# A Swin pair on one core: image loads and stores issued from ScalarE instead of SyncE

## The chip, the cores and the metric

One Trainium2 chip, one core. The metric is device time in microseconds (us) of the whole program, as the median of several runs; beside it stands one profiled execution, whose rows are quoted below.

## What is computed

Two Swin transformer blocks are applied to 32 images of 192 channels and 32 x 32 pixels, float32, given and returned as (image, channel, row, column). Cut to what matters:

```python
x = x.transpose(0, 2, 3, 1)
shortcut = x
xn = layernorm(x)                                # over the 192 channels
xs = roll(xn, (-4, -4))                          # windows of 8 x 8 pixels
qkv = windows(xs) @ qkv_w + qkv_b                # 12 heads of 16
attn = softmax(q * 16 ** -0.5 @ k + bias + mask)
x = shortcut + roll(merge(attn @ v) @ proj_w + proj_b, (4, 4))
x = x + gelu(layernorm(x) @ fc1_w + fc1_b) @ fc2_w + fc2_b
```

The first block has the relative bias and the shift mask; the second has neither and is otherwise the same, with its own weights.

## The kernel before, in words

An image is held in SBUF as `x_img`, 96 partitions x 2 x 1024 float32, 768 KB; the finished image is gathered in `y_img`, of the same shape. The 1024 pixels make 8 tiles of 128 tokens (two windows each). There are 2 blocks x 8 tiles x 32 images = 512 visits of a tile, in groups of four, and `group_order` interleaves them: (image, block 0, first half), (previous image, block 1, first half), (image, block 0, second half), (previous image, block 1, second half). Every 16 visits the pattern repeats, with the next image.

The program is a software pipeline written out by hand. `run` (L253) calls a function `slot(s)` on each engine for s from -4 to 524; in slot s an engine works on several visits at different stages: the scores of visit s, the transposes of probabilities of s - 1, the projection of s - 3, the norm of s + 3 or s - 3, and a quarter of the MLP of an older group of four (`mlp_phase`, L100). Engines are tied by semaphores alone (`when`, L230: wait until stage `name` has been done for visit n), so they drift against each other: ScalarE and PE can be in slot s + 1 while SyncE is in slot s.

Between the engines run four DMA transposes per visit, all issued by SyncE (SP), in this order in each slot (L372 to L379): `qk_turn(s + 1)` (L369, q and k for the scores, tile `qkt`), `norm1_turn(s + 3)` (L346, `xt`, input of the qkv product), `norm2_turn(s - 3)` (L354, `ht`, input of the MLP), `o_turn(s - 1)` (L361, `ot`, input of the projection). Behind them, in two slots out of 16, stand the transfers of whole images: a load of the next image into `x_img` (L328), once POOL has copied the last tile of the present image out of it (`x_ordered`), and a store of `y_img` (L331), once ScalarE has put the last tile into it (`y_ready`). Those two are also in SP's one DMA queue.

On PE the scores of visit n begin at L485 (block 0) or L494 (block 1) and wait for `qkt`; the qkv product's q and k part is L436 with 384 columns and waits for `xt`; the v part is L469 and stands right ahead of the scores.

On ScalarE (ACT), slot s holds in this order: two or more GELUs in some slots, `norm2_hi` (L644), the copy of a new tile (L639), `v_hi` (L660), `p_hi` (L671), `y_evac` (L700, block 1's results into `y_img`), `exp` (L665), `qk_hi(s + 2)` (L651, two activations), and in every fourth slot GELUs around these.

POOL's `order_next` (L1065) is the reader of `x_img`: it waits for the load of its image and, four tiles in one group and four in another, copies it into windows.

Of the kernel before, what the change touches and what calls it, by code (L numbers as in the profile page):

```python
# [44 lines left out]
IMAGES, C, SIDE = 32, 192, 32  # L45
# [5 lines left out]
TILES = SIDE * SIDE // TOK  # L51
# [30 lines left out]
def visit(n):  # L82

    image, layer, half = GROUPS[n // GROUP]
    return image, layer, half * GROUP + n % GROUP


def rank(n):

    image, _, t = visit(n)  # L90
    return image * TILES + t
# [39 lines left out]
def swin_program(nc, x, layers, rel_bias, ident_in, q_mask_in, k_mask_in, out):  # L131
    H2 = C // 2
    with ExitStack() as ctx:
# [41 lines left out]
        x_img = sb("x_img", [H2, 2, SIDE * SIDE], F32)  # L175
# [51 lines left out]
        x_loaded = sem("x_loaded")  # L227
# [22 lines left out]
        def live(n):  # L250
            return 0 <= n < TOTAL
# [18 lines left out]
        @block.sync  # L270
        def _(sp):
            span = 2 * WS - 1

            def column(v, a, n):
                return v[a:a + n].rearrange("(c a) -> c a", a=1)

            def norm_columns(l, i, v):

                for dst, src in ((cols[:, l, i, 0:1], column(v, 0, 128)), (cols[0:CB, l, i, 1:2], column(v, 128, CB)),
                                 (cols[CB:128, l, i, 1:2], column(v, 0, CB)), (cols[:, l, i, 2:3], column(v, CB, 128))):  # L280
                    sp.dma_start(dst, src).then_inc(norm_in[l], 16)

            def weight_rows(j, v, n):

                for dst, src in ((stage[:, j % 2, 0, 0:n], v[0:128, :]), (stage[0:CB, j % 2, 1, 0:n], v[128:C, :]),
                                 (stage[CB:128, j % 2, 1, 0:n], v[0:CB, :]), (stage[:, j % 2, 2, 0:n], v[CB:C, :])):
                    sp.dma_start(dst, src).then_inc(w_in[j], 16)

            for l, L in enumerate(layers):
                for i, name in enumerate(("g1", "b1", "g2", "b2")):  # L290
                    norm_columns(l, i, L[name])
                for k, (name, n) in enumerate((("wqkv", 3 * C), ("wproj", C), ("wfc1", HID), ("wfc2", 0))):
                    j = 4 * l + k
                    if j >= 2:
                        sp.wait_ge(made, j)
                    if n:
                        weight_rows(j, L[name], n)
                    else:
                        sp.dma_start(stage[:, j % 2].rearrange("p a n -> p (a n)")[:, 0:HC * C]
                                     .rearrange("p (m c) -> p m c", m=HC),  # L300
                                     L[name].rearrange("(m p) c -> p m c", p=128)).then_inc(w_in[j], 16)
                    if k == 0:
                        for i, (bias, m) in enumerate((("bqkv", 3 * C), ("bproj", C), ("bfc2", C))):
                            o = (0, 3 * C, 4 * C)[i]
                            sp.dma_start(row[:, o:o + m], L[bias].rearrange("(a c) -> a c", a=1)).then_inc(w_in[j], 16)
                        sp.dma_start(vcol[:, 0:1], column(L["bqkv"], 2 * C, 128)).then_inc(w_in[j], 16)
                        sp.dma_start(vcol[0:CB, 1:2], column(L["bqkv"], 2 * C + 128, CB)).then_inc(w_in[j], 16)
                    if k == 2:
                        sp.dma_start(b_fc1[l][:, :], L["bfc1"].rearrange("(m p) -> p m", p=128),
                                     allow_slow_non_contiguous=True).then_inc(w_in[j], 16)  # L310
                    if j == 0:
                        sp.dma_start(ident[:, :], ident_in).then_inc(const_in[0], 16)
                        sp.dma_start(x_img[:, :, :], x[0].rearrange("(k p) h w -> p k (h w)", k=2)).then_inc(x_loaded, 16)
                    if j == 1:

                        for w in range(2):
                            for qr in range(WS):
                                src = bass.AP(tensor=rel_bias.tensor, offset=rel_bias.offset + qr * span * HEADS,
                                              ap=[[HEADS, WS], [span * HEADS, WS], [1, WS * HEADS]])
                                p0 = w * WIN + qr * WS  # L320
                                sp.dma_start(rel[p0:p0 + WS, :, :].rearrange("p (a b) h -> p a (b h)", a=WS), src)\
                                    .then_inc(const_in[2], 16)
                        sp.dma_start(q_mask[:, :], q_mask_in).then_inc(const_in[1], 16)
                        sp.dma_start(k_mask[:, :, :], k_mask_in).then_inc(const_in[1], 16)

            def load(image):

                sp.dma_start(x_img[:, :, :], x[image].rearrange("(k p) h w -> p k (h w)", k=2)).then_inc(x_loaded, 16)  # L328

            def store(image):  # L330
                sp.dma_start(out[image].rearrange("(k p) h w -> p k (h w)", k=2), y_img[:, :, :])\  # L331
                    .then_inc(y_stored, 16)

            when(sp, "x_ordered", TILES - 1)
            load(1)

            def slot(s):
                def ge(name, n):
                    when(sp, name, n)
                    sp.nop(nofuse=True)  # L340

                def norm1_turn(n):

                    ge("lo1", n)
                    ge("v_mm", n - 4)
                    sp.dma_start_transpose(xt[:, n % 4], xs[:, 0, n % 2].rearrange("p a c -> p (a c)"))\  # L346
                        .then_inc(LANDED["xt_in"][n % 2], 16)

                def norm2_turn(n):

                    ge("lo2", n)
                    ge("fc1", (n // GROUP - 2) * HC + HC - 1)
                    tok = slice((n % GROUP) * TOK, (n % GROUP + 1) * TOK)
                    sp.dma_start_transpose(ht[:, n // GROUP % 2, :, tok], xs[:, 1, n % 2].rearrange("p a c -> p (a c)"))\  # L354
                        .then_inc(LANDED["ht_in"][n % 2], 16)

                def o_turn(n):

                    ge("o_lo", n)
                    ge("pr", n - 2)  # L360
                    sp.dma_start_transpose(ot[:, n % 2], os[:, n % 2].rearrange("p a c -> p (a c)"))\  # L361
                        .then_inc(LANDED["ot_in"][n % 2], 16)

                def qk_turn(n):

                    ge("qk_lo", n)
                    ge("mask_set", n)
                    ge("s_mm", n - 2)
                    sp.dma_start_transpose(qkt[:, n % 2], qk[:, n % 2].rearrange("p h s d -> p (h s d)"))\  # L369
                        .then_inc(LANDED["qkt_in"][n % 2], 16)  # L370

                if live(s + 1):  # L372
                    qk_turn(s + 1)
                if live(s + 3):
                    norm1_turn(s + 3)
                if live(s - 3):
                    norm2_turn(s - 3)
                if live(s - 1):
                    o_turn(s - 1)  # L379
                if live(s + 10) and visit(s + 10)[1:] == (0, TILES - 1) and rank(s + 10) + 1 < IMAGES * TILES and s + 10 >= TILES:  # L380
                    ge("x_ordered", rank(s + 10))
                    load(rank(s + 10) // TILES + 1)
                if live(s - 9) and visit(s - 9)[1:] == (1, TILES - 1):
                    ge("y_ready", rank(s - 9))
                    store(rank(s - 9) // TILES)

            run(slot)
            sp.wait_ge(y_stored, 16 * IMAGES)
            sp.wait_ge(x_loaded, 16 * IMAGES)
# [239 lines left out]
        def _(act):  # L629
            copy = nc.scalar.activation  # L630
            act.wait_ge(made, 1 + 4 * LAYERS)

            def slot(s):
                def ge(name, n):
                    when(act, name, n)
# [56 lines left out]
                def y_evac(n):  # L692

                    image, _, t = visit(n)
                    ge("otr", rank(n))
                    if t == 0 and image > 0:
                        act.wait_ge(y_stored, 16 * image)
                    tile = ps_tr[0:H2, 0:2 * TOK].rearrange("p (k t) -> p k t", k=2)
                    for win, img in box_pairs(t, tile, y_img[:, :, :]):
                        last = copy(img, win, ACT.Copy)  # L700
                    last.then_inc(S["y_ready"], 1)
# [34 lines left out]
                    gelu(1)  # L736
                if last_block and place == 2:
                    y_evac(p * GROUP + 1)

            run(slot)  # L740


# [426 lines left out]
```

## Time and profile before

| | us |
|---|---|
| median of 3 runs | 4975.95 |
| lowest, highest run | 4972.98, 4988.05 |
| the profiled execution's own time | 4969.82 |
| its span | 4967.9 |

| engine | busy, us | share of the span |
|---|---|---|
| PE, matmuls | 4324.0 | 87% |
| PEld, weight loads | 3040.0 | 61% |
| DVE (VectorE) | 3374.5 | 68% |
| POOL (GpSimd) | 3008.3 | 61% |
| ACT (ScalarE) | 2772.6 | 56% |

A matmul counts as busy while it is in the pipeline, and weight loads overlap matmuls. The share is a mean over the span. Register, branch, semaphore and DMA-issuing instructions do not count as busy; the time of a DMA issue on SP stands in its own rows. A "wait" row names the instruction that ended an idle stretch.

### The profile page before, as it was taken

How to read it: one execution, taken by the hardware profiler on the slowest of the kernel's cores; microseconds unless marked ns; L12 is line 12 of the kernel's file. 1: busy time of each engine (PE TensorE's matmuls, PEld its weight loads, DVE VectorE, ACT ScalarE, POOL GpSimd, SP SyncE). 2: the span in 40 equal slices, each digit the busy share in tenths (PEclk: the TensorE clock that was granted, in tenths of full speed). 3: DMA queues.
4: the chain of work that ended last, by engine and by line, in shares of the span. 5: the costliest groups of instructions: out<-in, count | busy, mean ns of one | idle time of the engine just before them, and what ended most of it. 6: DMA issues, size and time to landing. Idle time of an engine off the chain costs nothing.

```text
span 4967.9 us, 174574 instructions
## 1 busy us (share of the span) xinstructions
PE 4324.0 (87%) x66384; PEld 3040.0 (61%) x66384; DVE 3374.5 (68%) x9081; ACT 2772.6 (56%) x5921; POOL 3008.3 (61%) x6254
## 2 busy tenths in 40 slices
PE   4888888988888988888889888888888888898987
PEld 2566665666666666666666666666566666666665
DVE  5666666767666767666666666766676666676765
ACT  1555555655555555555556555555555565555554
POOL 4666655666666666666566666665665665666654
PEclk9999999999999999999999999999999999999999
DMA  4444454445454444454454454444444544544442
GB/s 94 83 83 85 83 87 83 81 87 93 78 88 91 81 86 84 87 84 81 87 93 76 87 89 83 87 82 88 85 83 87 91 78 86 91 81 87 85 82 59
DMA packets 1467388, 420.49 MB, mean 85 GB/s; under 512 B 1450295, under 2 KB 1452731, under 8 KB 1466557
## 3 DMA queue, kind: packets, MB, share of 16 engines
q1 hardware_dynamic: 1466556, 409.32, 45.8%
q8 instruction: 532, 8.72, 0.7%
q14 instruction: 300, 2.45, 0.2%
HBM read 31.56 MB, written 25.17 MB: 11 GB/s over the span
## 4 chain that ended last, share of the span: by engine, by line
PE 46%; DMA 15%; DVE 10%; POOL 10%; issue 8%; SPq 8%; ACT 2%; POOLq 0%; DVEq 0%; ACTq 0%
PE ps_s L557 12%; DMA qkt<-qk 10%; PE bank L569 8%; PE bank L436 7%; PE bank L531 4%; POOL hid L1083 4%; DVE smax L880 3%; PE ps_t L514 3%; DMA xt<-xs 3%; DVE hid L918 3%; SPq L346 3%; PE ps_s L503 2%; POOL xs L1076 2%; PE bank L469 2%; PE ps_s L494 2%
## 5 line engine op out<-in xcount | busy, mean ns | idle before, releaser
L1022 POOL TENSOR_TENSOR rstd<-vare,half 128x2 f32<-128x2 f32 x518 | 360.1, 695 | 1081.2 <-DVE vare L858 1081.2
L918 DVE TENSOR_TENSOR hid<-hid 128x512 f16<-128x512 f32 x768 | 600.8, 782 | 528.5 <-POOL hid L1083 507.4
L557 PE MATMUL ps_s<-ht,w_fc 128*128 128x512 f16 x3840 | 878.7, 381 | 17.3 <-DMA ht<-xs 7.3
L569 PE MATMUL bank<-w_fc,hid 128*128 128x192 f16 x9216 | 851.0, 247 | 7.8 <-DVE hid L918 5.6
L880 DVE TENSOR_REDUCE smax<-ps_s 128x12 bf16<-128x768 f32 x512 | 488.2, 954 | 512.6 <-PE ps_s L494 499.7
L569 PEld LDWEIGHTS bank<-w_fc,hid 128*128 128x128 f16 x9216 | 774.1, 98 | 82.6 <-issue 55.9
L671 ACT ACTIVATE pt<-ps_t 128x768 f16<-128x768 f32 x512 | 415.4, 811 | 677.6 <-PE ps_t L514 674.6
L1083 POOL TENSOR_SCALAR hid<-hid 128x512 f16<-128x512 f32 x768 | 564.0, 734 | 310.6 <-ACT hid L679 309.1
L679 ACT ACTIVATE hid<-ps_s,b_fc 128x512 f32<-128x512 f32 x768 | 530.2, 690 | 342.4 <-PE ps_s L557 167.4
L557 PEld LDWEIGHTS ps_s<-ht,w_fc 128*128 128x128 f16 x3840 | 361.7, 98 | 459.9 <-issue 63.6
L436 PE MATMUL bank<-w_qkv,xt 128*128 128x384 f16 x2560 | 544.3, 346 | 47.6 <-DMA xt<-xs 45.2
L660 ACT ACTIVATE v_blk<-bank 64x192 f16<-64x192 f32 x1024 | 334.8, 327 | 325.7 <-PE bank L469 318.9
L651 ACT ACTIVATE qk<-bank 128x384 f16<-128x384 f32 x1024 | 447.8, 494 | 96.3 <-PE bank L438 93.8
L885 DVE TENSOR_TENSOR pt<-ps_t,pt 128x768 f16<-128x768 f32 x512 | 489.6, 956 | 16.3 <-issue 1.1
L665 ACT ACTIVATE p_tok<-ps_s 128x768 f32<-128x768 f32 x512 | 417.0, 814 | 134.4 <-PE ps_s L503 134.4
L514 PE MATMUL ps_t<-ident,p_tok 128*128 128x128 f32 x3072 | 487.7, 299 | 0.2 <-issue 0.2
L864 DVE SCALAR_TENSOR_TENSOR qk<-bank,qk 128x192 f16<-128x192 f32 x1024 | 316.6, 351 | 216.6 <-ACT qk L651 216.6
L644 ACT ACTIVATE xs<-xn 128x192 f16<-128x192 f32 x512 | 184.9, 361 | 450.2 <-POOL xn L1028 449.2
L436 PEld LDWEIGHTS bank<-w_qkv,xt 128*128 128x128 f16 x2560 | 256.8, 103 | 270.2 <-issue 129.6
L531 PEld LDWEIGHTS bank<-v_blk,pt 128*64 128x64 f16 x18432 | 332.9, 112 | 118.9 <-issue 118.9
L485 PE MATMUL ps_s<-bias_tab,pair_ident 128*128 128x384 f16 x512 | 142.0, 363 | 296.1 <-DMA qkt<-qk 282.6
L503 PE MATMUL ps_s<-smax,neg_ident 128*128 128x384 bf16 x1024 | 277.4, 355 | 132.5 <-DVE smax L880 129.3
(113 smaller groups left out, 7717.5 us busy)
## 6 DMA issues: line engine op xcount, KB each, us to landing
x_img<-in_x_dram SPq DMA_DIRECT2D x32, 768.0 KB, 5.9
out_dram<-y_img SPq DMA_DIRECT2D x32, 768.0 KB, 5.7
xt<-xs SPq DMA_TRANSPOSE x512
qkt<-qk SPq DMA_TRANSPOSE x512, 3.8
ot<-os SPq DMA_TRANSPOSE x512, 2.4
ht<-xs SPq DMA_TRANSPOSE x512, 2.3
stage<-in_L_conv_fc_w_dram SPq DMA_DIRECT2D x2, 384.0 KB, 4.0
stage<-in_L_conv_w_fc_dram SPq DMA_DIRECT2D x2, 384.0 KB, 4.5
```

The costliest lines, as they stand in the source:

```text
L436: last = mm(dst, blocks[:, blk, :], w[:, part, n0:n1], start=(i == 0), stop=(i == 4 and bias is None))
L514: last = nc.tensor.transpose(ps_t[:, g // 3, (g % 3) * TOK:(g % 3 + 1) * TOK], p_tok[:, n % 2, g].rearrange("p a k -> p (a k)"), ident[:, :])
L531: last = mm(ps_o[rows, g * 2 * VW:(g + 1) * 2 * VW].rearrange("p (a d) -> p a d", a=2), pt[:, n % 2, ps, g, rows], v_blk[:, n % 2, vs, :, ...
L557: last = mm(ps_s[:, u % 2, :], w_fc1[layer][:, part, m * 128:(m + 1) * 128], ht[:, p % 2, blk, :], start=(i == 0), stop=(i == 4))
L569: mm(bank[:, 0:C], hid16[:, hs, m, tok], w_fc2[layer][:, ws, m, :], start=(m == 0 and i == 0), stop=False)
L651: last = copy(qk[:, n % 2, i * HEADS:(i + 1) * HEADS, places, :], src.broadcast_to([128, HEADS, 2, HD]), ACT.Copy, scale=UNSCALE)
L665: nc.scalar.activation(p_tok[:, n % 2].rearrange("p g a k -> p a g k"), ps_s[:, :, 0:PAIRS * WIN].rearrange("p a (g k) -> p a g k", g=PAIR ...
L679: nc.scalar.activation(hid[:, u % 2, :], ps_s[:, u % 2, :], ACT.Gelu, bias=b_fc1[layer][:, m:m + 1], scale=UNSCALE).then_inc(S["gelu"], 1)
L880: v.tensor_reduce(smax[:, n % 2], ps_s[:, :, 0:PAIRS * WIN].rearrange("p a (g k) -> p a g k", g=PAIRS), AX.X, ALU.max).then_inc(S["max_don ...
L885: v.tensor_tensor(pt[:, n % 2, 1].rearrange("p (b g) t -> p b (g t)", b=2), ps_t[:, :, 0:3 * TOK], pt[:, n % 2, 0].rearrange("p (b g) t -> ...
L918: v.tensor_tensor(hid16[:, 1, m, :], hid[:, u % 2, :], hid16[:, 0, m, :], ALU.subtract)\
L1083: g_.tensor_scalar(hid16[:, 0, m, :], hid[:, u % 2, :], 1.0, 0.0, ALU.mult, ALU.add)\
```

## The change

`load` and `store` move from SP's program into ACT's, with the same transfers and the same semaphores. In ACT's slot they stand at the very end. A load is issued in the slot after the one that held it on SP (s + 9 in place of s + 10); a store in the slot of the same number. The first load inside the program, that of image 1 ahead of the loop, and that of image 0 stay on SP. SP still waits for all loads and stores at the end.

```diff
@@ SP @@
-            def store(image):
-                sp.dma_start(out[image].rearrange("(k p) h w -> p k (h w)", k=2), y_img[:, :, :])\
-                    .then_inc(y_stored, 16)
-
...
-                if live(s + 10) and visit(s + 10)[1:] == (0, TILES - 1) and rank(s + 10) + 1 < IMAGES * TILES and s + 10 >= TILES:
-                    ge("x_ordered", rank(s + 10))
-                    load(rank(s + 10) // TILES + 1)
-                if live(s - 9) and visit(s - 9)[1:] == (1, TILES - 1):
-                    ge("y_ready", rank(s - 9))
-                    store(rank(s - 9) // TILES)
-
@@ ACT @@
+            def load(image):
+
+                act.dma_start(x_img[:, :, :], x[image].rearrange("(k p) h w -> p k (h w)", k=2)).then_inc(x_loaded, 16)
+
+            def store(image):
+                act.dma_start(out[image].rearrange("(k p) h w -> p k (h w)", k=2), y_img[:, :, :])\
+                    .then_inc(y_stored, 16)
+
...
                 if last_block and place == 2:
                     y_evac(p * GROUP + 1)
+                if live(s + 9) and visit(s + 9)[1:] == (0, TILES - 1) and TILES <= s + 9 and visit(s + 9)[0] + 1 < IMAGES:
+                    ge("x_ordered", rank(s + 9))
+                    act.nop(nofuse=True)
+                    load(visit(s + 9)[0] + 1)
+                if live(s - 9) and visit(s - 9)[1:] == (1, TILES - 1):
+                    ge("y_ready", rank(s - 9))
+                    act.nop(nofuse=True)
+                    store(visit(s - 9)[0])
```

The place of a load in SP's queue, before: between the `ot` transpose that ends a slot and the `qkt` transpose that begins the next. In brackets are the semaphores waited for.

```order
L354 DMA_TRANSPOSE ht<-xs 128x3x128 [waits lo2,fc1]
L361 DMA_TRANSPOSE ot<-os 128x3x128 [waits o_lo,pr]
L328 DMA x_img<-in_x_dram 96x2x1024 [waits x_ordered]
L369 DMA_TRANSPOSE qkt<-qk 128x12x128 [waits qk_lo,mask_set,s_mm]
L346 DMA_TRANSPOSE xt<-xs 128x3x128 [waits lo1,v_mm]
```

The same place now; the lines of SP's part are lower by four.

```order
L350 DMA_TRANSPOSE ht<-xs 128x3x128 [waits lo2,fc1]
L357 DMA_TRANSPOSE ot<-os 128x3x128 [waits o_lo,pr]
L365 DMA_TRANSPOSE qkt<-qk 128x12x128 [waits qk_lo,mask_set,s_mm]
L342 DMA_TRANSPOSE xt<-xs 128x3x128 [waits lo1,v_mm]
L350 DMA_TRANSPOSE ht<-xs 128x3x128 [waits lo2,fc1]
```

Only L328 is gone; a store (L331) stood at the like place in its slot and is gone as well.

ScalarE at a load, now: from the copy of the probabilities to the v copy of the next slot. (Before, the rows were the same without the DMA, with lines higher by three.)

```order
L668 ACTIVATE pt<-ps_t 128x768 [waits tp]
L662 ACTIVATE p_tok<-ps_s 128x2x6x64 [waits shift]
L648 ACTIVATE qk<-bank 128x12x32 [waits qkt_in_even,qk_mm]
L648 ACTIVATE qk<-bank 128x24x16
L624 DMA x_img<-in_x_dram 96x2x1024 [waits x_ordered]
L641 ACTIVATE xs<-xn 128x192 [waits ht_in_odd,ln2]
L657 ACTIVATE v_blk<-bank 64x12x16 [waits v_mm]
```

The load came in between the second activation of `qk_hi` and the activation of `norm2_hi`.

ScalarE at a store, now: the last pieces of the finished image, the exponential, the q and k copies, the store.

```order
L697 ACTIVATE y_img<-bank 96x2x4x8
L697 ACTIVATE y_img<-bank 96x2x4x4 x2
L662 ACTIVATE p_tok<-ps_s 128x2x6x64 [waits shift]
L648 ACTIVATE qk<-bank 128x12x32 [waits qkt_in_even,qk_mm]
L648 ACTIVATE qk<-bank 128x24x16
L627 DMA out_dram<-y_img 96x2x1024 [waits y_ready]
L641 ACTIVATE xs<-xn 128x192 [waits ht_in_odd,ln2]
```

The store too stands behind `qk_hi` and ahead of the next slot's `norm2_hi`.

## Rows read from the trace of the kernel before

**Rows 1.** The page: the chain that ended last, by engine.
```profile
PE 46%; DMA 15%; DVE 10%; POOL 10%; issue 8%; SPq 8%; ACT 2%; POOLq 0%; DVEq 0%; ACTq 0%
```
**Rows 2.** Waits over the whole span: us in total, times, longest us.
```profile
PE ps_s L485 <- DMA qkt<-qk: 282.6, 105, 5.7
```
**Rows 3.** DMA issues: count, KB each, median us from issue to landing.
```profile
x_img<-in_x_dram SPq DMA_DIRECT2D x32, 768.0 KB, 5.9
out_dram<-y_img SPq DMA_DIRECT2D x32, 768.0 KB, 5.7
qkt<-qk SPq DMA_TRANSPOSE x512, 3.8
...
ht<-xs SPq DMA_TRANSPOSE x512, 2.3
...
ident<-in_const_ident_dram SPq DMA_DIRECT2D x1, 64.0 KB, 2.2
```
**Rows 4.** Timeline of SP at a load: start us, duration us, instruction.
```profile
2291.00 0.52 SPq L328 DMA_DIRECT2D x_img<-in_x_dram  x1
2291.72 1.61 SPq L369 DMA_TRANSPOSE qkt<-qk  x1
```
**Rows 5.** Timeline of PE there; in brackets idle before, and what ended it.
```profile
2293.74 0.62 PE L469 MATMUL bank<-w_qkv,xt 128*64 128x96 f16 x20
2299.96 0.80 PE L485 MATMUL ps_s<-bias_tab,pair_ident 128*128 128x384 f16 x2 [5.60 <-DMA qkt<-qk]
```
**Rows 6.** One microsecond there: five engines' busy us, PEclk, DMA share, GB/s.
```profile
2299.00:2300.00 1.00, 0.04 (x1) 0.07 (x2) 0.00 (x0) 0.00 (x0) 0.02 (x1) 0.50 0.94 132
```
**Rows 7.** Timeline of SP around a store.
```profile
2354.62 1.44 SPq L369 DMA_TRANSPOSE qkt<-qk  x1
2358.81 1.18 SPq L346 DMA_TRANSPOSE xt<-xs  x1
...
2362.74 0.52 SPq L331 DMA_DIRECT2D out_dram<-y_img  x1
2363.46 4.11 SPq L369 DMA_TRANSPOSE qkt<-qk  x1
```
**Rows 8.** Timeline of PE around the store.
```profile
2362.12 0.97 PE L436 MATMUL bank<-w_qkv,xt 128*128 128x384 f16 x5
...
2366.04 0.62 PE L469 MATMUL bank<-w_qkv,xt 128*64 128x96 f16 x20
2371.05 0.80 PE L485 MATMUL ps_s<-bias_tab,pair_ident 128*128 128x384 f16 x2 [4.40 <-DMA qkt<-qk]
```
**Rows 9.** Timeline of SP: q(16), q(24), q(472), q(488), q(496).
```profile
218.51 1.44 SPq L369 DMA_TRANSPOSE qkt<-qk  x1
...
291.49 1.44 SPq L369 DMA_TRANSPOSE qkt<-qk  x1
...
4539.69 1.44 SPq L369 DMA_TRANSPOSE qkt<-qk  x1
...
4689.51 1.43 SPq L369 DMA_TRANSPOSE qkt<-qk  x1
...
4760.88 1.43 SPq L369 DMA_TRANSPOSE qkt<-qk  x1
```
**Rows 10.** Timeline of ACT around the store.
```profile
2355.52 0.92 ACT L651 ACTIVATE qk<-bank 128x384 f16<-128x384 f32 x2
2358.19 0.36 ACT L644 ACTIVATE xs<-xn 128x192 f16<-128x192 f32 x1 [1.75 <-POOL xn L1028]
```
**Rows 11.** One microsecond ahead of the store, columns as in rows 6.
```profile
2358.00:2359.00 1.00, 1.00 (x26) 0.66 (x23) 0.91 (x3) 0.48 (x2) 1.00 (x3) 1.00 0.00 0
```
**Rows 12.** Timeline of ACT at the load.
```profile
2291.00 0.87 ACT L651 ACTIVATE qk<-bank 128x384 f16<-128x384 f32 x2 [0.99 <-PE bank L438]
2292.41 0.36 ACT L644 ACTIVATE xs<-xn 128x192 f16<-128x192 f32 x1 [0.54 <-POOL xn L1028]
```

## The prediction

> **What bounds the kernel now.** I read the page first, for the chain that ended last: 46% of it is TensorE (PE), 15% DMA, 8% SP's own queue [rows 1]. So no engine is simply full; transposes by DMA stand between ScalarE and VectorE on one side and PE on the other, and part of the path is made of them. The waits say which: PE stood 282.6 us before the first matmul of the scores (L485) for the transposed q and k, in 105 waits, 2.7 us each on average and 5.7 at most [rows 2]. The DMA list gives the normal times from issue to landing: 3.8 us for the qkt transpose, 2.3 for the small ht one, 5.9 for an image load, 5.7 for a store [rows 3]. Then I looked at one load and one store on SP and on PE, to see whether those waits belong to them.
>
> I write q(n) for the qkt transpose of tile visit n, counted from 0. It is issued in slot n-1 of SP's program and used by scores(n).
>
> *The load.* SP issues it at 2291.00 and q(11 mod 16) behind it at 2291.72 [rows 4]. PE is through with the v product at 2293.74 + 0.62 = 2294.36 and idles 5.60 us for that qkt transpose, to 2299.96 [rows 5]. The transpose thus landed some 8.2 us after its issue where 3.8 is normal. While PE stood, its granted clock went from full speed to 0.50, the 1.2 GHz level, in 2299:2300 [rows 6].
>
> *The store.* SP issues it at 2362.74 and q(2 mod 16) at 2363.46, whose issue alone takes 4.11 us [rows 7]. PE is ready at 2366.04 + 0.62 = 2366.66 and idles 4.40 us [rows 8].
>
> **What the two transfers cost today.** The program holds two controls of its own. The first store comes in slot 32, so the half period q(16) to q(24) has none: 291.49 - 218.51 = 72.98 us. The last load comes in slot 473, so q(488) to q(496) has none: 4760.88 - 4689.51 = 71.37 us [rows 9]. Together 144.35. An ordinary period of 16 slots, the mean of the 28 from q(24) to q(472), is (4539.69 - 291.49) / 28 = 151.72 us [rows 9]. Load and store thus cost 7.37 us per image in time, less than the 10.0 us that PE idles at them, because other waits lie beside these. I split it as the PE waits are split, 5.60 to 4.40: 4.13 us for a load, 3.24 for a store. With 30 loads and 31 stores inside the loop (the first in-program load stays on SP ahead of the loop, the last store has no transpose behind it) the whole is 30 x 4.13 + 31 x 3.24 = 224 us. That is the ceiling of the gain; each control is a single stretch, so it is good to perhaps 1.5 us per image, or 45 us in all.
>
> **The change, part by part.**
>
> *Removed from SP:* 61 DMA issues and their waits in the loop. From a load's issue to the next is 2291.72 - 2291.00 = 0.72 us [rows 4]; SP issues back to back there, so q(11) and q(2) start 0.72 us sooner. This is inside the price above.
>
> *The store on ScalarE (ACT).* It now stands behind qk_hi of the same slot. That activation pair ends at 2355.52 + 0.92 = 2356.44 [rows 10], so the store goes out 6.3 us earlier than today. Its wait, y_ready, is for ACT's own evacuation earlier in the slot and costs nothing. It lands about 2356.44 + 5.7 = 2362.1. The transpose ahead, q(1), was issued at 2354.62 and lands by 2358.4 [rows 3, 7]; the DMA engines carry nothing in 2358:2359 [rows 11]. So the store falls mostly into a hole. What it can touch is xt(3), issued at 2358.81 [rows 7], normally landed by 2361.1 (as ht, 2.3 us) and needed at 2362.12, when PE starts the qk product [rows 8]: 1.0 us of cover. In the worst case xt(3) lands about 1.0 us late for PE, in the best there is no wait; I take 0.5. q(2) is then alone: issued 2362.74, landed 2366.5, PE ready at 2366.66, no wait. Gain of a store 3.24 - 0.5 = 2.7 us, times 31 = 85 us (bounds 2.2 and 3.24: 69 and 100).
>
> *The load on ACT.* In the code it is one slot later, but ACT is at that point a slot ahead of what SP is issuing: its qk_hi pair ends at 2291.00 + 0.87 = 2291.87 [rows 12], 0.9 us after today's issue. The order against q(11) flips: q(11) at 2291.00, the load 0.9 us behind. Undisturbed, q(11) lands at 2294.8, 0.4 us after PE is ready. But the two are in flight together now. How the DMA engines share themselves between two queues no row of before shows, so I bound it. Best case: q(11) goes first and the load costs nothing; gain 4.13. Worst case: the load's whole moving time falls into q(11). That time is the landing of 768 KB less the landing of the 64 KB identity, 5.9 - 2.2 = 3.7 us [rows 3]; q(11) lands at 2298.5, PE waits 4.15 us instead of 5.60, gain 1.45. I take the middle, 2.8, since q(11) is nearly a microsecond ahead and PE's clock may not drop in a shorter wait: 30 x 2.8 = 84 us (bounds 44 and 124).
>
> *Added to ACT:* 61 issues of 0.52 us [rows 4], and a wait of the load for x_ordered, which POOL gave a slot earlier. Behind the load stands norm2's activation, which today starts at 2292.41, 0.54 us after the pair ends [rows 12]; behind the store the same one, with 1.75 us of idle time before it [rows 10]. Both issues fit into ACT's idle time, so I cost them at nothing. If the cover were gone it would be 61 x 0.52 = 32 us.
>
> *Deadlines.* The loaded image is first read by POOL four slots after the new place, 4 x 151.72 / 16 = 38 us for 5.9; the stored one is overwritten later still. Nothing is late there.
>
> Sum: 85 + 84 = 169 us, against the profiled execution's own 4969.82 us: 4801, rounded 4800. That execution lies 6.1 us (0.12%) under the median of the runs shown. Runs of this kernel differ by some 0.3%, about 15 us, which is what I call no change.
>
> **The rivals.**
>
> *The load passes q(11) whole.* A load moves as few large pieces per engine, the transpose as many small ones; if the engines take turns piece by piece, all of the load is through before q(11) is, and the worst case above holds each time: 44 us from the loads in place of 84, 4969.8 - 44 - 85 = 4841. That both are in flight together speaks for it, q(11)'s head start against. Chance 0.22. Such turns are the rule of the Trainium skill, page "DMA: Bandwidth & Descriptors", section "Queues, rings and completion order": an engine drains one packet of several descriptors from a queue and goes to the next queue with work. No row here shows it yet.
>
> *Everything is won.* Neither transfer meets a transpose that PE needs at once: 4969.8 - 224 = 4746 us. The 6.3 us hole speaks for it at the store; that load and q(11) must overlap speaks against. Chance 0.18.
>
> *The collision stays and only issue time is saved.* DMA engines are shared whichever queue feeds them; if both transfers push a needed transpose back as far as today, 61 x 0.72 = 44 us remain: 4926. The store's place speaks against, the load's for. Chance 0.09. This is also what the Trainium skill states, page "DMA: Bandwidth & Descriptors", section "Issuing engines are not separate DMA queues": DMAs from several engines run on the same 16 DMA engines and interleave, and issuing from another engine saves only sequencer time.
>
> *It does not matter.* Behind the removed waits stands another chain of the same length, such as POOL's and VectorE's norms: 4970. The two controls, which are shorter, speak against. Chance 0.05.
>
> *Slower: ACT is held at its DMA issue.* The row of q(2) shows that an issue can take 4.11 us where descriptors pile up [rows 7]. Were ACT held as long at each, norm2's activation would start 2296.0 instead of 2292.41 at the load, 3.6 us late, and 2360.55 instead of 2358.19 at the store, 2.4 late: 6.0 us per image, on an engine that every stage passes. With the worst collisions (2.7 left at the load, 1.0 at the store) that is 9.7 us per image in place of 7.4, some 2.3 x 30.5 = 70 us more: 5040. It decides from a hold of about 3 us at each. Against it: ACT's new queue has no backlog, and the load's issue on SP took 0.52. Chance 0.06.
>
> **How the numbers follow.** The forecast has 0.40, with its own range 4746 to 4857 from the bounds, in which the first rival lies too. The predicted time is its value, 4800. The range adds the full gain and the looseness of the controls below, 4730, and above a load and a store that each keep part of today's collision, 4890; issue time only, no change and slower, together 0.20, stay outside. Faster by over 0.3%: 0.40 + 0.22 + 0.18 + 0.09 = 0.89; within 0.3%: 0.05; slower: 0.06.
>
> **What would show it.** Right: PE's wait before L485 for qkt falls from 282.6 us to under 150; q(2) lands in about 3.8 us and its issue takes 1.4; load and store are issued right behind the second activation of the qk copy, and the gap to ACT's next activation grows by nothing that PE sees. Wrong: a load behind which q(11) still lands 8 us after issue; a new wait of PE for xt behind the store of more than 1 us; DMA rows on ACT that last several microseconds; or a period of 16 slots that stays at 151.7 us.

## The result, and the profile after

The changed kernel takes 5010.41 us (median of 17 runs, 4988.52 to 5033.6) against 4982.7 us of the kernel before in the same sessions: a ratio of 1.0065, 95% interval 1.005 to 1.0079. The profiled execution took 5009.68 us with a span of 5007.1, 39 us more than that of before. The change makes the kernel slower by two thirds of a per cent, where 3.4% faster was forecast. One of the 17 runs of before took 6353 us and is left out of the ratio, which goes by all the other runs and not by the two medians.

Four views of the kernel after answer to rows of before. The waits of PE (engine, line, waited for: us in total, times, longest; L474 is L485 of before, L425 is L436, L458 is L469, L503 is L514):

```profile
PE ps_s L474 <- DMA qkt<-qk: 281.4, 108, 6.2
...
PE bank L425 <- DMA xt<-xs: 60.9, 70, 4.6
...
PE bank L425 <- DMA ot<-os: 10.9, 9, 4.0
```

PE waits for the q and k transposes as long as before (281.4 us, [rows 2] 282.6). The page's chain that ended last, by engine, and then the DMA issues (count, KB, median us to landing):

```profile
PE 44%; DMA 18%; POOL 10%; issue 9%; DVE 8%; SPq 7%; ACT 2%; DVEq 0%; POOLq 0%; ACTq 0%
```
```profile
out_dram<-y_img ACTq DMA_DIRECT2D x32, 768.0 KB, 7.2
x_img<-in_x_dram ACTq DMA_DIRECT2D x30, 768.0 KB, 6.7
...
qkt<-qk SPq DMA_TRANSPOSE x512, 3.8
```

DMA has 18% of the chain in place of 15% [rows 1]; a store lands after 7.2 us instead of 5.7, a load after 6.7 instead of 5.9 [rows 3]. The two whole transfers became slower in a queue of their own. PE's wait for `xt` was 45.2 us before and is 60.9 now.

The place of a store, on ACT (its activations and, as ACTq, its DMA issues: start us, duration us):

```profile
2370.31 0.86 ACT L662 ACTIVATE p_tok<-ps_s 128x768 f32<-128x768 f32 x1
2370.89 0.34 ACTq L627 DMA_DIRECT2D out_dram<-y_img  x1
2371.00 0.93 ACT L648 ACTIVATE qk<-bank 128x384 f16<-128x384 f32 x2
2373.66 0.36 ACT L641 ACTIVATE xs<-xn 128x192 f16<-128x192 f32 x1 [1.74 <-POOL xn L1033]
```

The store stands in the program behind both activations of `qk_hi` (L648), and yet it is issued at 2370.89, while the exponential runs and before `qk_hi` has begun. So ScalarE's issuing side was at the DMA while three activations ahead of it in the program were still running or to come: being behind them in the program did not hold the DMA until they were done. SP and PE around it:

```profile
2370.09 1.42 SPq L365 DMA_TRANSPOSE qkt<-qk  x1
2374.28 1.18 SPq L342 DMA_TRANSPOSE xt<-xs  x1
...
2378.88 1.42 SPq L365 DMA_TRANSPOSE qkt<-qk  x1
```
```profile
2373.71 0.62 PE L458 MATMUL bank<-w_qkv,xt 128*64 128x96 f16 x20
2378.38 0.80 PE L474 MATMUL ps_s<-bias_tab,pair_ident 128*128 128x384 f16 x2 [4.06 <-DMA qkt<-qk]
```

The store is 0.80 us behind q(1) (2370.09), not 1.82 as in the prediction, and q(1), which was safe before, now lands 8.2 us after its issue; PE waits 4.06 us for it. q(2), at 2378.88, is well again: its issue takes 1.42 us instead of 4.11 [rows 7]. The wait moved from q(2) to q(1). Over the run this offset is nearly constant: of the 30 stores that meet a q(1), 28 are issued 0.04 to 0.80 us behind it and two 0.3 and 0.4 us ahead of it; the median is 0.80 us. The median landing of these q(1) is 8.5 us after their issue, where it was 3.7 before.

What the engines do meanwhile is in the packet records of the trace. Counted in half microseconds over all 16 engines, with the time of the first instruction as zero:

```
from us   queue 1, 256 bytes   queue 10, 4096 bytes
2371.50    417                    0
2372.00    417                    0
2372.50    244                    1
2373.00    129                   21
2373.50     42                   21
2374.00     38                   29
2374.50     37                   39
2375.00     29                   37
2375.50     36                   37
2376.00    269                    7
```

Queue 1 is SP's (transposes, pieces of 256 bytes), queue 10 is ACT's (the store, one row of 4096 bytes a piece). As soon as the store is there, transposes fall from 417 pieces to some 37 per half microsecond, about as many as the store's pieces: one for one. In bytes that is 1 to 16. When the store's first piece moved, at 2372.92, 341 of q(1)'s 1536 pieces were still to come. This is the turn-taking that the Trainium skill describes in "DMA: Bandwidth & Descriptors", section "Queues, rings and completion order"; where it speaks of several descriptors per turn, the counts here fit turns of a single piece. The store has 192 pieces, 12 per engine if they are spread evenly. In turns of a dozen the transposes would stand near zero while these 12 pass; they run on at 29 to 42 per half microsecond. The records do not name the engine of a piece, so this is read from the sums.

The load, at 2308.17, is issued as early against its activations, and practically together with q(11) (SP 2308.21):

```profile
2310.86 0.62 PE L458 MATMUL bank<-w_qkv,xt 128*64 128x96 f16 x20
2316.72 0.80 PE L474 MATMUL ps_s<-bias_tab,pair_ident 128*128 128x384 f16 x2 [5.25 <-DMA qkt<-qk]
```

PE waits 5.25 us, where it waited 5.60 [rows 5].

To put numbers on load and store apart, I measure from the starts of the `qkt` transposes, as in the prediction. The *store half* is q(n) to q(n + 8) for n = 32, 48, ..., the *load half* the same for n = 24, 40, ..., 28 stretches each; the *period* is q(24) to q(472) by 28. For the kernel after, the ends of the period are

```profile
291.42 1.42 SPq L365 DMA_TRANSPOSE qkt<-qk  x1
...
4572.99 1.42 SPq L365 DMA_TRANSPOSE qkt<-qk  x1
```

(4572.99 - 291.42) / 28 = 152.91 us, 1.19 more than before. The store half went from 75.90 to 77.11, the load half from 75.82 to 75.80. So the loss is at the store, 1.2 us per image or 36 us in the 30 images whose store meets a `qkt` transpose, and the load gave nothing.

The single store shown, 4.06 us against 4.40, is kinder than the mean. Summed over the 28 store halves, PE waits 5.19 us for `qkt` in each, where it was 4.42; with the smaller waits its idle time is 1.24 us longer per half, which is the whole loss. In the load half the wait for `qkt` did fall, from 4.77 to 3.78 us, but those for `xt` and `ot` rose from 0.60 to 1.21 and from 0.09 to 0.35.

### The profile page after: what moved, and what is told of

Same layout as the page of the kernel before. It is cut to its first block, busy times and chain, and to the rows that moved or that the text cites. A ratio compares the mean times of both kernels' runs of the same rounds, so it can differ in the third digit from the quotient of the medians.

```text
span 5007.1 us, 174574 instructions
## 1 busy us (share of the span) xinstructions
PE 4329.4 (86%) x66384; PEld 3054.7 (61%) x66384; DVE 3375.6 (67%) x9081; ACT 2774.4 (55%) x5921; POOL 2996.3 (60%) x6254
## 4 chain that ended last, share of the span: by engine, by line
PE 44%; DMA 18%; POOL 10%; issue 9%; DVE 8%; SPq 7%; ACT 2%; DVEq 0%; POOLq 0%; ACTq 0%
DMA qkt<-qk 12%; PE ps_s L546 12%; PE bank L558 9%; PE bank L425 6%; PE bank L520 4%; DMA xt<-xs 4%; POOL hid L1088 3%; PE ps_t L503 3%; DVE smax L885 3%; SPq L342 2%; SPq L357 2%; POOL xs L1081 2%; PE ps_s L483 2%; PE ps_s L492 2%; DVE hid L923 2%
## 5 line engine op out<-in xcount | busy, mean ns | idle before, releaser
L558 PE MATMUL bank<-w_fc,hid 128*128 128x192 f16 x9216 | 878.2, 252 | 7.5 <-DVE hid L923 5.5
L558 PEld LDWEIGHTS bank<-w_fc,hid 128*128 128x128 f16 x9216 | 798.6, 100 | 83.1 <-issue 50.9
L425 PE MATMUL bank<-w_qkv,xt 128*128 128x384 f16 x2560 | 521.8, 336 | 61.9 <-DMA xt<-xs 60.9
L648 ACT ACTIVATE qk<-bank 128x384 f16<-128x384 f32 x1024 | 448.1, 495 | 83.5 <-PE bank L427 80.8
L503 PE MATMUL ps_t<-ident,p_tok 128*128 128x128 f32 x3072 | 486.2, 299 | 0.1
L425 PEld LDWEIGHTS bank<-w_qkv,xt 128*128 128x128 f16 x2560 | 249.3, 100 | 269.6 <-issue 120.6
L474 PE MATMUL ps_s<-bias_tab,pair_ident 128*128 128x384 f16 x512 | 141.8, 362 | 295.3 <-DMA qkt<-qk 281.4
L492 PE MATMUL ps_s<-smax,neg_ident 128*128 128x384 bf16 x1024 | 267.1, 344 | 141.5 <-DVE smax L885 138.5
```

Source lines behind the costliest of these rows:

```text
L425: last = mm(dst, blocks[:, blk, :], w[:, part, n0:n1], start=(i == 0), stop=(i == 4 and bias is None))
L503: last = nc.tensor.transpose(ps_t[:, g // 3, (g % 3) * TOK:(g % 3 + 1) * TOK], p_tok[:, n % 2, g].rearrange("p a k -> p (a k)"), ident[:, :])
L558: mm(bank[:, 0:C], hid16[:, hs, m, tok], w_fc2[layer][:, ws, m, :], start=(m == 0 and i == 0), stop=False)
L648: last = copy(qk[:, n % 2, i * HEADS:(i + 1) * HEADS, places, :], src.broadcast_to([128, HEADS, 2, HD]), ACT.Copy, scale=UNSCALE)
```

## The experiments

The table gives all of them beside both kernels; the ratio is to the kernel before in the same session, with its 95% interval. Period and halves are of one profiled execution each, and between kernels whose load is untouched the load half differs by up to 0.9 us, so smaller differences there say nothing.

| kernel | ratio | interval | period | store half | load half |
|---|---|---|---|---|---|
| before | 1 | | 151.72 | 75.90 | 75.82 |
| after | 1.0065 | 1.005 to 1.0079 | 152.91 | 77.11 | 75.80 |
| e1, store alone on ACT | 1.0074 | 1.005 to 1.0098 | 154.06 | 77.33 | 76.73 |
| e2, load alone on ACT | 0.999 | 0.9973 to 1.0008 | 151.82 | 75.57 | 76.25 |
| e3, both wait for qk_hi | 0.975 | 0.973 to 0.9771 | 148.10 | 72.66 | 75.44 |
| e4b, both in quarters | 0.9719 | 0.9694 to 0.9744 | 147.91 | 74.51 | 73.40 |
| e5, on SP behind qkt | 0.974 | 0.9725 to 0.9755 | 147.63 | 73.61 | 74.02 |
| e6, no transfers | 0.9425 | 0.9409 to 0.9441 | 142.74 | 71.14 | 71.60 |
| e9, store in 128-byte pieces | 0.9874 | 0.9852 to 0.9896 | 149.60 | 74.23 | 75.36 |
| e10, quarters that wait | 0.9603 | 0.9587 to 0.9619 | 145.44 | 72.23 | 73.21 |
| e11, store whole, load in quarters, both wait | 0.9592 | 0.9567 to 0.9618 | 146.14 | 72.85 | 73.29 |

**Which of the two moves costs: e1 and e2.** In e1 the load's call goes back into SP's slot, in e2 the store's.

> Only the store moves to ScalarE, the load stays on SyncE as before. Theory A (ScalarE's sequencer issues the store while the exponential still runs, 0.8 us behind q(1), and the DMA engines then take turns piece by piece, so the store cuts into q(1) where before it stood ahead of q(2)): the whole loss sits at the store, period 16 slots 152.9 us, time 1.005 to 1.01 of before. Rival B (the loss comes from the load on ScalarE or from both together): 0.99 to 1.00 of before.

> Only the load moves to ScalarE, the store stays on SyncE. Theory A: the load's collision with q(11) is as dear as before, ratio 0.997 to 1.003. Rival B: the load carries the loss, ratio 1.005 to 1.01.

The store alone gives 1.0074, all of the loss, the load alone 0.999, no change. Both ratios are as theory A has them, and B is out. The period of e1, 154.06 us, is 1.2 above the expected one; 0.9 of it stands in the load half, where e1 is the same as before.

**Is it the 1 us by which the store is early: e3.** The two transfers stay on ACT, at the same place, and each waits for its slot's `qk_hi`, which holds it until the activations have really been done. The same two lines stand ahead of the load:

```diff
                     ge("y_ready", rank(s - 9))
+                    if live(s + 2):
+                        ge("qk_hi", s + 2)
                     act.nop(nofuse=True)
                     store(visit(s - 9)[0])
```

> Load and store on ScalarE, but both wait for qk_hi of their own slot to be finished, as the prediction had placed them. Theory A: the store goes out 1.8 us behind q(1) and misses nearly all of its packets; q(1) lands in 4 to 5 us instead of 8, the load is 1 us or more later against q(11): 2 to 4 us less per image and transfer, ratio 0.96 to 0.99 of before. Rival C (two queues with work slow each other wherever the transfer falls, or ScalarE is what suffers): ratio 1.00 to 1.01.

Ratio 0.975: one wait more at each transfer, and 2.5% faster than before, 3.1% faster than the changed kernel. A store of this kernel, on ACT, on SP and on PE:

```profile
2300.93 0.93 ACT L648 ACTIVATE qk<-bank 128x384 f16<-128x384 f32 x2
2301.93 0.34 ACTq L627 DMA_DIRECT2D out_dram<-y_img  x1
```
```profile
2300.02 1.42 SPq L365 DMA_TRANSPOSE qkt<-qk  x1
2304.20 1.19 SPq L342 DMA_TRANSPOSE xt<-xs  x1
```
```profile
2303.63 0.62 PE L458 MATMUL bank<-w_qkv,xt 128*64 128x96 f16 x20
2304.18 0.50 PE L474 MATMUL ps_s<-bias_tab,pair_ident 128*128 128x384 f16 x2
...
2308.76 0.97 PE L425 MATMUL bank<-w_qkv,xt 128*128 128x384 f16 x5 [1.07 <-DMA xt<-xs]
```

The store now follows q(1) by 1.91 us. PE starts the scores without a wait; what is left is 1.07 us for xt. That is the picture that the prediction had drawn for the change itself, with its upper bound of 1.0 us at xt, and the store half is 75.90 - 72.66 = 3.24 us shorter. Two of this kernel's 30 stores went out only 0.32 and 0.80 us behind q(1) all the same, and there q(1) again landed 7.8 and 7.5 us after its issue. Summed over the run, PE's waits for qkt nearly halve, those for xt grow (60.9 in the kernel after):

```profile
PE ps_s L474 <- DMA qkt<-qk: 154.7, 92, 6.9
...
PE bank L425 <- DMA xt<-xs: 87.0, 96, 4.6
```

The load half gained little (75.44), 0.4 us where 2 to 4 were expected: the offset of a load against q(11) varies from one image to the next, from 0.05 to 4.32 us here, so that 11 of 30 loads still go out within 1 us of it. This makes a scale of its own. I sorted the loads by their offset and took the four gaps q(9) to q(13) around each; the kernel before has 40.5 us there, e6, without transfers, 35.8:

| load issued after q(11) by | kernel after | e3 |
|---|---|---|
| under 1.0 us | 40.8 (21 loads) | 42.0 (11) |
| 1.0 to 3.65 us | 38.1 (8) | 38.0 (15) |
| over 3.65 us | 41.8 (1) | 41.4 (4) |

In the first row of the kernel after, 8 of the 21 are issued up to 0.8 us ahead of q(11). A load that goes out 1 to 3.65 us behind q(11) costs about 2.3 us, one that goes out with it 5 or more. This is a sorting of what happened, with bounds drawn after the fact, and not an experiment. One of the good ones in the kernel after, on SP, ACT and PE:

```profile
2924.56 1.42 SPq L365 DMA_TRANSPOSE qkt<-qk  x1
```
```profile
2925.97 0.32 ACTq L624 DMA_DIRECT2D x_img<-in_x_dram  x1
```
```profile
2929.21 0.50 PE L474 MATMUL ps_s<-bias_tab,pair_ident 128*128 128x384 f16 x2
```

With 1.41 us between the issues there is no wait before L474 at all. What an offset above 3.65 us hits is not settled; the `ht` and next `qkt` transposes are issued then, and with five loads I leave it there.

**Is it the turns: e9.** `y_img` gets rows of 36 pixels of which 32 are stored, so that a piece is 128 bytes and not 4096. The store then takes two issues, one after the other. Everything else, the store's early issue too, stays as in the changed kernel.

```diff
-        y_img = sb("y_img", [H2, 2, SIDE * SIDE], F32)
+        y_img = sb("y_img", [H2, 2, SIDE, SIDE + 4], F32)
...
-                act.dma_start(out[image].rearrange("(k p) h w -> p k (h w)", k=2), y_img[:, :, :])\
-                    .then_inc(y_stored, 16)
+                for k in range(2):
+                    act.dma_start(out[image].rearrange("(k p) h w -> k p h w", k=2)[k], y_img[:, k, :, 0:SIDE])\
+                        .then_inc(y_stored, 16)
```

> The changed kernel with y_img's rows padded from 32 to 36 pixels, so that the store, at the same place 0.8 us behind q(1), moves 128-byte pieces instead of 4 KB pieces (in two issues of 96 x 32 x 32). Theory A (turns piece by piece): the pieces of q(1) still outstanding then wait for as many small pieces, not for large ones: q(1) lands within 5 us and most of the store's 4 us collision goes, though the store lasts longer and slows xt and ht a little: ratio 0.975 to 0.995 of before. Rival E (a store in flight delays the transposes for its own time whatever its pieces are): ratio 1.005 to 1.03.

Ratio 0.9874, 1.9% below the changed kernel, as A has it. q(1) is issued at 2029.23 and the store at 2030.03, 0.80 us behind as in the kernel after, but PE's wait is 0.28 us:

```profile
2033.74 0.48 PE L474 MATMUL ps_s<-bias_tab,pair_ident 128*128 128x384 f16 x2 [0.28 <-DMA qkt<-qk]
...
2038.41 0.97 PE L425 MATMUL bank<-w_qkv,xt 128*128 128x384 f16 x5 [1.17 <-DMA xt<-xs]
```

PE's mean wait for q(1) over 28 store halves is 1.34 us, where the kernel after has 4.60. Here 166 pieces of q(1) were still to come when the first small piece moved, and q(1) landed 1.5 us after that piece; in the kernel after they were 341, and q(1) landed 5.3 us after the first 4 KB piece. So at the same offset it is mainly the size of the pieces that made the overlap dear, and not the overlap. That fewer pieces of q(1) were left here is a part of it that no run separates. Small pieces have a price of another kind: the second half's issue holds ACT for 3.87 us, the very event of the prediction's last rival, and it idles 3.57 us.

```profile
2030.03 0.61 ACTq L628 DMA_DIRECT2D out_dram<-y_img  x1
...
2030.67 3.87 ACTq L628 DMA_DIRECT2D out_dram<-y_img  x1
2034.64 0.36 ACT L642 ACTIVATE xs<-xn 128x192 f16<-128x192 f32 x1 [3.57 <-issue]
```

**Does it need a queue of its own: e5.** The kernel before, with both transfers still whole on SP, moved by one place, from ahead of the qkt transpose to behind it (the old lines at the end of the slot are gone):

```diff
                 if live(s + 1):
                     qk_turn(s + 1)
+                if live(s + 9) and visit(s + 9)[1:] == (0, TILES - 1) and rank(s + 9) + 1 < IMAGES * TILES and s + 9 >= TILES:
+                    ge("x_ordered", rank(s + 9))
+                    load(rank(s + 9) // TILES + 1)
+                if live(s - 10) and visit(s - 10)[1:] == (1, TILES - 1):
+                    ge("y_ready", rank(s - 10))
+                    store(rank(s - 10) // TILES)
```

> The kernel before, all in SyncE's one queue, with load and store one place later: behind the qkt transpose in place of ahead of it. Theory A (what counts is which transpose the transfer meets, not whose queue it is in): q(2) and q(11) land in 3.8 us, the xt behind them is late by up to 4 us, of which PE sees 1 to 2: gain 5 to 6 us per image, ratio 0.96 to 0.975. Rival D (the gain of the run with waits for qk_hi needs the second queue): ratio 0.99 to 1.00.

Ratio 0.974, the same as e3 to within the intervals, with nothing on ACT. D is out, though the gain of 151.72 - 147.63 = 4.1 us per image is under the 5 to 6 expected. The waits say what changed hands:

```profile
PE bank L436 <- DMA xt<-xs: 153.6, 108, 4.6
...
PE ps_s L485 <- DMA qkt<-qk: 79.1, 103, 2.6
```

qkt from 282.6 to 79.1, xt from 45.2 in the kernel before to 153.6. A transfer behind q meets xt instead, which PE needs later. This agrees with what the Trainium skill states on the page "DMA: Bandwidth & Descriptors", section "Issuing engines are not separate DMA queues": all DMAs run on the same 16 engines and interleave, whoever issues them.

**How much there was to win: e6.** Loads of images 2 to 31 and stores of images 0 to 30 are left out; the rest is computed, on stale images.

> The kernel before without loads of images 2 to 31 and without stores of images 0 to 30 (left out: those transfers; all else is computed, on stale images). It measures the ceiling that the prediction took from two stretches, 224 us: ratio 0.955 by that. If the stretches misled, the ratio is above 0.975.

0.9425: the ceiling is 284 us (4978.73 - 4694.27) and not 224. Store 75.90 - 71.14 = 4.76 us per image, load 75.82 - 71.60 = 4.22. The two control stretches of the prediction understated it, all at the store: 72.98 in its control, 71.14 here, and 71.37 against 71.60 at the load.

Not all of this is waiting. PE's busy time is 4227.5 us here and was 4324.0 before, for the same 66384 matmuls, and its mean granted clock 0.990, where it was 0.961. After the wait of rows 8 the granted clock stays at 0.50, the 1.2 GHz level, from 2371 to 2377, and the same six matmuls take nearly twice as long as in the next slot:

```profile
2372.24 1.54 PE L514 MATMUL ps_t<-ident,p_tok 128*128 128x128 f32 x6
...
2380.97 0.88 PE L514 MATMUL ps_t<-ident,p_tok 128*128 128x128 f32 x6
```

Of the store's 4.8 us per image, 2.6 are idle time of PE and 2.1 longer busy time; of the load's 4.2, 3.2 and 1.0.

**A better version: e4b, e10, e11.** Each transfer in four, of 256 pixels, one per slot (e4b; the load's part is shown):

```diff
+            def load(image, part):
+                c = slice(part * PX, (part + 1) * PX)
+                act.dma_start(x_img[:, :, c], x[image].rearrange("(k p) h w -> p k (h w)", k=2)[:, :, c]).then_inc(x_loaded, 16)
...
+                for part in range(PARTS):
+                    m = s + 9 - part
+                    if live(m) and visit(m)[1:] == (0, TILES - 1) and TILES <= m and visit(m)[0] + 1 < IMAGES:
+                        if part == 0:
+                            ge("x_ordered", rank(m))
+                            act.nop(nofuse=True)
+                        load(visit(m)[0] + 1, part)
```

> Load and store on ScalarE, each cut into four transfers of 256 pixels (192 KB, rows of 1 KB), one per slot in four slots that follow each other (the last two images' stores go out at once). Theory A (the engines take turns piece by piece, so a transfer holds up whatever transposes are in flight for its own moving time): a quarter holds up the transposes for at most 1 us, and most of that is covered by slack: ratio 0.955 to 0.98 of before. Rival C (two queues slow each other at each meeting, and ScalarE pays for four times as many issues): ratio above 1.00.

> Load and store on ScalarE in quarters, one per slot, and every quarter waits for qk_hi of its slot. Theory A: the quarters then start 1 us or more behind a qkt transpose and hit only xt, ht and ot, each by about 1 us, so that most of the 4.8 and 4.2 us of an image's store and load go: period 144 to 146.5 us, ratio 0.950 to 0.967. If the waits hold ScalarE up more than they help: 0.97 to 0.98.

> The store whole, the load in quarters, both on ScalarE behind a finished qk_hi. If the costs of the two transfers add as the half periods do (72.7 us for a whole store that waits, 73.4 for a load in quarters): period 146.1, ratio 0.96 to 0.966 of before.

The last two images' stores are an exception because the same kernel without it, e4, deadlocks and has no time: ScalarE waits there for a whole store of which quarters stand behind that wait in its own program.

Quarters alone give 0.9719, with 120 loads and 128 stores; more meetings cost less, as theory A has it. Quarters that also wait for `qk_hi` give 0.9603, and the whole store with the load in quarters 0.9592, at the period of 146.1 that adding the halves had given. Both beat both kernels: e11 by 4.1% (4781.43 against 4982.45 us), which is seven tenths of the ceiling (201 of 284 us). They are the same within their intervals. e10 is as expected; e11's ratio lies a hair under the 0.96 to 0.966 expected.

## Why the prediction was wrong

*What bounds the kernel, and what the two transfers cost.* Right in kind: q(2) and q(11) behind a store and a load are what PE waits for, and e5 wins 2.6% by moving just that. Too small in size: 7.37 us per image by the controls, 8.98 by e6. And 30 stores have a `qkt` transpose to meet, not 31.

*"It now stands behind qk_hi of the same slot. That activation pair ends at ... 2356.44 ..., so the store goes out 6.3 us earlier than today."* This is the step that failed and that decided the sign. The prediction let the DMA wait for the activations ahead of it in ScalarE's program. It did not; it went out 1.0 us before the end of `qk_hi`'s pair (2370.89 against 2371.93), and so 0.80 us behind q(1) and not 1.8. The distance mattered because q(1)'s pieces were not yet through. With the wait of e3 the step becomes true, and the store gains 3.24 us per image where 2.7 was forecast. That this is just the forecast's upper bound is luck: by e6 the store cost 4.76, so 1.5 are left, where the forecast left 0.5.

*"The transpose ahead, q(1), was issued at 2354.62 and lands by 2358.4."* I treated transposes ahead of a transfer as safe, as they were in the one queue of before. Between these two queues they are not, and this was written out as a rival for the load, yet not applied to the store: no rival has a store that hits q(1). The q(1) ahead of a store landed 3.7 us after its issue when both were in SP's queue, and 8.5 now (medians of 30).

*The load, gain 2.8 with bounds 1.45 and 4.13.* Measured 0.0 (75.82 to 75.80; e2 0.999). The order flipped only in part: of 30 loads 8 are still issued up to 0.8 us ahead of q(11), 13 up to 1 us behind it and 9 later. And the "worst case" was not the worst: it let the load move at its own speed, 3.7 us, and q(11) land after 7.5 us. In the turns both are slowed: the load lands after 6.7 us instead of 5.9, and q(11), at the 21 loads within 1 us of it, 8.3 us after its issue. Nor had the forecast a term for `xt` and `ot` behind the load, whose waits took back 0.9 us of the 1.0 won at `qkt`. The first rival, that the load passes q(11) whole, was the right one in its mechanism and still 1.5 us too kind.

*0.72 us of SP's issue time.* Most of it is there, in the gap from q(10) to q(11), 7.90 before and 7.32 now in the mean of 28, and is lost again in the next, 7.89 to 8.33.

*ACT's issues at nothing, deadlines, the last rival.* The issues take 0.32 to 0.41 us each, under the 0.52 allowed, and ACT's gap to its next activation behind the store shown is 1.74 us, as it was (1.75), and 0.52 behind the load shown (0.54). Nothing was late. The slower side came, but not by ACT being held at its issue, as the rival had it.

*The signs.* q(2) does land in 3.7 us and its issue takes 1.42, as forecast for the right case; PE's wait for `qkt` stayed at 281.4 us and q(11) still lands over 8 us after its issue at many loads, as written down for the wrong one.

*Why a store that hits q(1) is dearer by 1.2 us than one that hits q(2).* PE's idle time accounts for all of it, as its busy time per store half is the same, 67.5 us. For `qkt` PE waits 0.77 us more per half: 4.60 at q(1) now, where it was 4.21 at q(2), and 0.59 at q(3), where it was nothing. In e6, with no transfer at all, PE still waits 0.18 at q(1), 0.61 at q(2) and 0.37 at q(3). So the long wait at q(2) had those at q(2) and q(3) inside it, and the one at q(1) leaves that at q(3) to be paid. This reading is argued from the waits; no run isolates it. The rest is in small waits for VectorE and others.

## What to carry to other kernels

Here a transfer of 768 KB held up the small transposes that shared the DMA engines with it by about 4 us: ask which of them a bulk transfer meets and how much cover that one has, before asking for another queue. In SP's own queue it delayed only what stood behind it; from ACT's queue it also delayed what was already in flight, since its 4 KB pieces took turns with pieces of 256 bytes. So place it behind the transfer that the critical engine needs next (0.974 in one queue, 0.975 in two), tie it by a semaphore to the event that you mean (place in ScalarE's program was not it), and cut it so that each part fits into the cover of what it meets (0.972 alone, 0.960 with the semaphore).

## What the runs showed of the hardware that I had not expected

ScalarE issued its DMA while an activation three places ahead was still running: 2370.89, inside the exponential of 2370.31 to 2371.17, ahead of two further activations. With the wait on its own `qk_hi` it went out 0.07 us after the pair's end (2301.86 to 2301.93).

Two queues took turns about one piece for one piece, 29 to 42 of 256 bytes against 21 to 39 of 4096 bytes in half a microsecond. And a DMA issue of 3072 small pieces right behind another such held ScalarE for 3.87 us, against 0.34 for the store of the whole image in 4 KB rows.
